# Reordering cross attention's first two rounds: one value product, the additions and the roundings change places

## The reference, cut to what matters

```python
x = x + _L2_ffn_ref(_layernorm(x), ...)      # F
x = x + _L3_xattn_ref(_layernorm(x), ctx_2048, ...)   # G

# F: rows quantised to 255 levels, ternary weights, a bias
scale = jnp.maximum(jnp.max(jnp.abs(x), -1, keepdims=True), eps) / 127.0
q_x = jnp.clip(jnp.round(x / scale), -128.0, 127.0) * scale
return jnp.einsum('bsi,oi->bso', q_x, q_w) + bias

# G: its input is normalised a second time, divided by four vectors of scales
# (for q, qx, k, v) and rounded to fp8; 8 groups g of two heads
ln_out = _ln(hidden_states, ln_w, ln_b)
q  = _ln(_fp8_linear_pertensor(ln_out, wq,  wq_scale,  q_in_scale), qln_w, qln_b)
k  = _ln(_fp8_linear_pertensor(ln_out, wk,  wk_scale,  k_in_scale), kln_w, kln_b)
v  =     _fp8_linear_pertensor(ln_out, wv,  wv_scale,  v_in_scale)
qx = _ln(_fp8_linear_pertensor(ln_out, wqx, wqx_scale, qx_in_scale), qxln_w, qxln_b)
kx, vx = jnp.split(jnp.einsum('bsi,oi->bso', cond, w_kv_x), 2, axis=-1)
cat = concatenate([_gqa(q, k, v), _gqa(qx, kx, vx)])
return jnp.einsum('bsi,oi->bso', _div_clamp_fp8(cat, proj_smooth), wproj) * ...
```

## Time and profile before

| | |
|---|---|
| median of 3 runs | 1086.16 us (1083.81 to 1086.54) |
| the profiled execution's own time | 1085.14 us |
| its span, first to last instruction | 1083.3 us |
| mean granted TensorE clock | 0.987 |
| busy: PE, DVE, ACT, POOL | 1021.9, 868.9, 621.1, 560.1 us |
| round 0's linear products start | 529.12 us |
| round 1's | 550.86 us |
| round 2's | 574.83 us |
| round 3's | 592.02 us |

### The profile page before, as it was taken

The page is one execution under the profiler, slowest core; times in us unless marked ns, Lnnn a source line. Parts: engine busy times, 40 slices in busy tenths (PEclk is TensorE's granted clock), DMA queues, the critical chain, the costliest instruction groups (busy, mean ns, idle before and its releaser), DMA issues.

```text
span 1083.3 us, 19032 instructions
## 1 busy us (share of the span) xinstructions
PE 1021.9 (94%) x6538; PEld 872.1 (80%) x6538; DVE 868.9 (80%) x2154; ACT 621.1 (57%) x1661; POOL 560.1 (52%) x409
## 2 busy tenths in 40 slices
PE   8999999999998899889877999999999999999988
PEld 7458888888887787556556888998889988998976
DVE  6467777767778867789999889888987889888885
ACT  1774444444333347777566756775767666675643
POOL 4247666678653233135156664656555664655540
PEclk9999999999999999899989999999999999999999
DMA  7002101011100012000001101020100101000201
GB/s 272 1 21 93 59 30 59 31 59 40 49 1 28 0 57 77 3 2 2 21 1 42 38 1 41 1 60 1 40 1 21 39 1 40 1 21 1 89 1 40
DMA packets 15007, 37.43 MB, mean 35 GB/s; under 512 B 1648, under 2 KB 6848, under 8 KB 14400
## 3 DMA queue, kind: packets, MB, share of 16 engines
q1 hardware_dynamic: 14912, 36.21, 10.1%
HBM read 35.16 MB, written 1.05 MB: 33 GB/s over the span
## 4 chain that ended last, share of the span: by engine, by line
PE 65%; DVE 20%; ACT 7%; issue 3%; POOL 3%; DMA 0%; DVEq 0%; SPq 0%; ACTq 0%; POOLq 0%
PE bank L743 16%; PE bank L765 8%; PE bank L2213 8%; PE bank L2190 8%; PE bank L2121 7%; PE bank L2096 3%; PE bank L2132 3%; ACT y L2338 3%; PE bank L1128 2%; DVE bst L249 1%; PE bank L2110 1%; DVE y L286 1%; PE bank L531 1%; DVE g_ql L2055 1%; PE bank L532 1%
## 5 line engine op out<-in xcount | busy, mean ns | idle before, releaser
L2338 ACT ACTIVATE y<-bank,g_mx 128x256 f32<-128x256 f32 x256 | 117.2, 484 | 97.8 <-DVE g_mx L2508 97.8
L2623 POOL TENSOR_TENSOR y<-y,g_sm 128x1024 f32<-128x1024 f32 x64 | 120.1, 1896 | 23.9 <-DVE g_sm L2521 23.9
L2599 POOL TENSOR_TENSOR g_c<-arena 128x1024 fp32r<-128x1024 f32 x30 | 64.1, 2135 | 116.4 <-DVE arena L2442 116.4
L2213 PE MATMUL bank<-arena 128*128 128x256 f32 x512 | 116.0, 379 | 0.0
L795 ACT ACTIVATE arena<-arena 128x512 f32<-128x512 f32 x64 | 40.4, 632 | 120.6 <-DVE arena L880 120.5
L2213 PEld LDWEIGHTS bank<-arena 128*128 128x128 f32 x512 | 94.9, 190 | 12.0 <-issue 0.2
L743 PE MATMUL bank<-b_yh,b_wh 128*128 128x512 f32 x256 | 100.6, 393 | 0.0
L743 PE MATMUL bank<-b_yl,b_wh 128*128 128x512 f32 x256 | 100.0, 390 | 0.0
L743 PE MATMUL bank<-b_yh,b_wl 128*128 128x512 f32 x256 | 99.7, 389 | 0.0
L2096 PE MATMUL bank<-cst,y 128*128 128x128 f32 x512 | 74.0, 277 | 17.9 <-DVE x L2430 14.7
L831 POOL TENSOR_TENSOR b_hl<-arena,b_hh 128x512 fp32r<-128x512 f32 x64 | 81.3, 1291 | 9.6 <-ACT b_hh L804 9.6
(11 more groups left out here) (387 smaller groups left out, 3140.0 us busy)
## 6 DMA issues: line engine op xcount, KB each, us to landing
arena<-in_dram SPq DMA_DIRECT2D x37, 512.0 KB, 3.6
arena<-in_dram SPq DMA_DIRECT2D x18, 256.0 KB, 4.0
arena<-in_dram SPq DMA_DIRECT2D x3, 1024.0 KB, 4.9
arena<-in_dram SPq DMA_DIRECT2D x2, 704.0 KB, 7.2
x<-in_dram SPq DMA_DIRECT2D x4, 256.0 KB, 5.4
cx<-in_dram SPq DMA_DIRECT2D x4, 256.0 KB, 5.5
cxT<-in_dram SPq DMA_DIRECT2D x4, 256.0 KB, 5.8
cx<-in_dram SPq DMA_DIRECT2D x1, 1024.0 KB, 8.2
```

The costliest lines, as they stand in the source:

```text
L2213: m = pe.matmul(o[:, st * 256:st * 256 + 256], g_t[:, c, st * P:st * P + P], keys, start=True, stop=True)
L2338: m = act.activation(g_p[:, c, st, :], o[:, st * 256:st * 256 + 256], ACT.Exp, bias=g_mx[j % 2][:, 2 * c + st:2 * c + st + 1], accum_out=g ...
L2599: pool.tensor_tensor(cat, g_o[j % 2], g_om, ALU.subtract).then_inc(s_gc, 1)
L2623: pool.tensor_tensor(pf, pf, sums, ALU.mult).then_inc(s_gp, 1)
```

## The change

Nothing is computed otherwise; instructions of rounds 0, 1 and (for one) 2 change places.

```diff
--- before.py
+++ after.py
@@ -1918,7 +1918,7 @@
         G_TRANSPOSES = (("pt", 0), ("tr", 0), ("pt", 1), ("tr", 2), ("tr", 1), ("pt", 2), ("pt", 3))
         CROSS = [tuple(("V", b, n // 2, n % 2) for n in range(4)) for b in range(B)]
         G_AHEAD = {0: CROSS[1], 1: (("G", "yt", 2),)}
-        G_EXTRA = {0: (("F", "t", 2), ("F", "o", 2)) + CROSS[2] + (("F", "t", 3), ("F", "o", 3)),
+        G_EXTRA = {0: (("F", "t", 2), ("F", "o", 2)) + CROSS[2][0:3] + (("F", "t", 3), CROSS[2][3], ("F", "o", 3)),
                    1: (("G", "yt", 3),) + CROSS[3]}
         for i in range(NG + 3):
             for what, c in G_TRANSPOSES:
@@ -2227,8 +2227,9 @@
                 if i == 0:
                     F_t_pe(pe, 2)
                     F_o_pe(pe, 2)
-                    cross_v_pe(pe, 2, g_wvx[:, 0, :], g_wvx[:, 1, :])
+                    cross_v_pe(pe, 2, g_wvx[:, 0, :], g_wvx[:, 1, :], range(3))
                     F_t_pe(pe, 3)
+                    cross_v_pe(pe, 2, g_wvx[:, 0, :], g_wvx[:, 1, :], (3,))
                     F_o_pe(pe, 3)
                 if i == 1:
                     yt_pe(pe, K_G, "G", (3,))
@@ -2323,8 +2324,9 @@
                                                  scale=row("s_v")), ("G", "kv", i, tt))
                 if i == 0:
                     F_qT_act(act, 2)
-                    cross_v_act(act, 2)
-                    split_p_act(act, 0)
+                    cross_v_act(act, 2, range(3))
+                    F_qT_act(act, 3)
+                    cross_v_act(act, 2, (3,))
                 if i == 1:
                     G_yt_act(act, 3)
                 if 0 <= i - 1 < NG:
@@ -2357,7 +2359,7 @@
                         G_ob_act(act, j, a)
 
                 if i == 0:
-                    F_qT_act(act, 3)
+                    split_p_act(act, 0)
                 if i == 1:
                     G_scale_act(act, 3)
                     cross_v_act(act, 3)
@@ -2510,8 +2512,11 @@
                 if i == 0:
                     ln_scale(dve, K_F, 3)
                     F_quant_dve(dve, V, 3)
-                if i in (1, 2):
-                    G_round_dve(dve, V, i + 1, (i - 1,))
+                    F_bias_dve(dve, V, 3)
+                if i == 1:
+                    G_round_dve(dve, V, 2)
+                if i == 2:
+                    G_round_dve(dve, V, 3, (1,))
                 for tt in range(2):
                     if 0 <= i - 1 < NG:
                         j = i - 1
@@ -2533,18 +2538,15 @@
                         empty(dve.tensor_tensor(g_n[:, tt * 5:tt * 5 + 4, :], o[:, :].rearrange("p (h d) -> p h d", d=P),
                                                 rs4, ALU.mult), ("G", "q", i, tt))
                 if i == 0:
-                    G_round_dve(dve, V, 1, (0,))
                     F_add_dve(dve, V, 2)
                     ln_open_batch(dve, V, 2)
+                    G_round_dve(dve, V, 1, (0,))
+                    ln_scale(dve, K_G, 2)
                     G_round_dve(dve, V, 1, (1,))
-                    ln_scale(dve, K_G, 2)
-                    F_bias_dve(dve, V, 3)
                     F_add_dve(dve, V, 3)
                     ln_open_batch(dve, V, 3)
                     split_p_dve(dve, 0)
                     ln_scale(dve, K_G, 3)
-                if i == 1:
-                    G_round_dve(dve, V, 2, (1,))
                 if i == 2:
                     centre_w_dve(dve, V, 1)
                 if i == 3:
@@ -2608,8 +2610,8 @@
                     C.sync()
                     pool.tensor_tensor(r_, r_, mhalf[:, 0:10], ALU.pow).then_inc(s_grs, 1)
                 if i == 0:
+                    ln_pool(pool, C, K_G, EPS, twice=True, batches=(2,))
                     G_round_pool(pool, 1, (0,))
-                    ln_pool(pool, C, K_G, EPS, twice=True, batches=(2,))
                     G_round_pool(pool, 1, (1,))
                     ln_pool(pool, C, K_G, EPS, twice=True, batches=(3,))
                 if i == 1:
```

## The result

Over 20 runs each, taken in turn, the changed kernel has a median of 1085.78 us (1084.81 to 1088.42) and the kernel before 1084.12 (1081.82 to 1086.98); the ratio is 1.0017, with a 95% interval of 1.0010 to 1.0024. So by the ratio the change costs 1.8 us (1.1 to 2.6): it is slower, and by less than 0.3%. The forecast was +2.3 us. Its 1088.4 us lay higher than the 1085.78 measured mainly because the kernel before's own median came down from 1086.16 in the three runs shown to 1084.12 in twenty.

The account below looks back on a forecast made before the run. PE was taken to bound the kernel, but not rounds 0 and 1, where DVE and POOL delay its start. 2.71 + 0 - 0.43 = +2.28 us, carried whole: 1088.4 us on the median, range 1084.4 to 1091.3.

Parts of the forecast that it names:

- First part, the row of DVE in round 0: Round 0: DVE's new order up to the second rounding delays POOL's subtractions and PE's round 1 start by 2.71 us.
- The products on PE and ACT: Rounds 0 and 1: PE's swapped products and ACT's split projection fall ahead of the wait for `g_xs`, so worth 0.
- The clock: Round 1's linear products: PE again at the low clock, the same 6.27 us, so 0; bounds 2.33 less, 0.3 more.
- Rival 2: PE's clock stays at 2.4 GHz into round 1's linear products; sum -1.3 us, 1084.8 us; chance 0.15.
- Second part, round 1: DVE's new order in round 1: last maximum to PE's round 2 start takes 13.00 us for 13.43, -0.43.
- The lock taken to the letter: DVE and POOL: an exclusive port lock blocks the later one for whole instructions; sum +3.4 us in place of +2.3.
- The carry: From round 2 on both orders are alike, so the +2.28 us reaches the end whole.
- Rival 3: PE's 14.7 us of slack behind 600 us absorbs the delay; 1086.2 us; chance 0.12.
- rival 1: Both locks cost in full and PE's clock falls again in round 1; +4.9 us, 1091.1 us; chance 0.25.
- The signs named beforehand: PE's round 1 products near 553.6 after about 5 us idle, transposes L340 near 547.8, round 2 near 577.1.

Follow-up runs that it names:

- e1: The changed kernel with the order of DVE and POOL in round 0 put back as before; ratio to the kernel before 0.9993 (0.9981 to 1.0004).
- e4: The kernel before with only the change's moves on PE and ACT; ratio to the kernel before 0.9989 (0.9979 to 1.0000).
- e3: The changed kernel with only batch 3's bias put back behind the second rounding; ratio to the kernel before 1.0008 (0.9997 to 1.0019).
- e5: The changed kernel with POOL's first pair of subtractions in round 1 moved behind its multiplications; ratio to the kernel before 1.0026 (1.0015 to 1.0037).
- e7: e6 with DVE also doing batch 2's second pair of subtractions in round 1; ratio to the kernel before 1.0014 (1.0003 to 1.0025).
- after_again: The changed kernel measured once more, nothing altered; ratio to the kernel before 1.0024 (1.0014 to 1.0034).
- e6: e1 with DVE doing batch 1's last two subtractions in round 0, batch 2's transposes and scaling later; ratio to the kernel before 1.0001 (0.9988 to 1.0014).
- e9: e8 with DVE also doing batch 1's second pair of subtractions in round 0, PE's order kept; ratio to the kernel before 0.9992 (0.9981 to 1.0002).
- e8: e1 with DVE doing batch 2's second pair of subtractions in round 1; ratio to the kernel before 0.9990 (0.9981 to 0.9999).

## Why the prediction was right

*First part, the row of DVE in round 0: predicted +2.71 us, measured +2.55.* The row itself is exact: 11.24 us for the 11.24 that the sum gives (539.70 to 550.94). Its scaling took 1.57 (1.56 expected) and the delayed first instruction 1.38 (0.42 + 0.95). The 0.15 that is missing lies behind it: POOL's last subtractions took 2.27 us and not 2.42, since DVE's next instructions, F's addition and moments, left them alone. That the loss comes from the order of DVE and POOL in round 0, and not from PE's and ACT's moves, is shown by e1, which takes PE's start back to 21.74, and by e4. That it is not the row's length alone is shown by e3: a row 0.74 us shorter brought PE's start forward by 0.35, since POOL's subtractions grew by 0.38.

*The products on PE and ACT: 0, right for the start of round 1.* F's last product starts 13.4 us behind round 0's products for 15.8, and all of it came back as idle time; in e4's trace the moves alone leave round 1's start at 21.74. What the term leaves out is the clock, through which e4 and e1 seem to win about 1 us over many executions; with the whole change the mean granted clock over twenty executions is 0.9885, so nothing of it is seen there.

*The clock: 0, measured +0.17.* Most of the linear products ran at 1.2 GHz, 6.44 us for 6.27. Rival 2, that the clock would stay high, did not come.

*Second part, round 1: predicted -0.43, measured -0.45.* The sum is right, its terms for the second rounding and for POOL are not. The second rounding took 4.19 us and not 3.81: both of POOL's subtractions hit it, 0.83 each, and I had taken 1.3 for the two. POOL's multiplications took 3.70 from start to start (3.74 in their row) for the 3.92 and its subtractions 2.27 for the 2.46. I had taken both from rows with a rounding of DVE's beside them; here two normalisations and a copy out of a PSUM bank stood beside the multiplications and took their usual 0.66 and 0.69, and of a rounding only the first instruction met the last subtraction (and took 1.03 for 0.42). The errors are +0.38 and -0.41. This is luck, and a better sum would have asked of each POOL duration as well what ran beside it in the old order.

*The lock taken to the letter*, that each of the two subtractions stops DVE for its whole length, would have given 2.27 us of delay; e5 measures 1.67. The rule of the Trainium skill ("SBUF — State Buffer", section "SBUF: two separate sides") holds in kind, as e5 and e7 show; its size here is 0.83 for a subtraction of 1.28. Of that, 0.29 us was over when DVE's instruction started (565.92 and 566.21); the other 0.16 is not explained.

*The carry: whole, right.* +2.27 at round 2, +2.33 at round 20, +2.32 at the end. Rival 3 is out. So is rival 1, which asked for steps of 2.9 and 0.5 us and a clock that falls again in round 1: the steps are 2.55 and -0.45, and the granted clock from 572.20 to 576.20 is 1.00.

*The signs named beforehand.* They are on the clock of the old trace, which this execution runs 0.87 us ahead of. With 0.87 added, the transposes L340 start at 547.68 (near 547.8 was named), round 1's products at 553.41 (near 553.6) after 5.10 us of waiting for POOL, and round 2's at 577.10 (near 577.1). `g_xs` of batch 1 was finished at 552.49 as read, and at 553.36 on the old clock, so not before 552.5. Maximum to start took 12.98 us, between 12 and 14.

*Level.* 2.55 + 0.17 - 0.45 = 2.27 us in the profiled executions; the ratio over all runs gives 1.8 (1.1 to 2.6), that of after_again 1.0024, or 2.6 us (1.5 to 3.7).

## What to carry to other kernels

When two chains end within 0.1 us of each other, moving an instruction ahead of the end of one lengthens that chain, however long the wait that it removes in the other; write both ends down before moving anything. The cost is up to the instruction's full length: the bias, 0.72 us in the row, was worth 0.35 at PE's start (e3). On VectorE and GpSimd a row's duration is a duration in company: before reusing it in another place, see what the other engine did beside it. And an order that makes TensorE early without making its next input early buys an idle stretch (4.13 us in e6, 2.96 in e9), which can be paid for a second time in the clock.

## What was not expected of the hardware

- TensorE's clock makes two executions of the same work differ by nearly as much as the change does. Ahead of round 0, where all kernels here are alike, PE idles 2.0 us before its transposes L340. In e1 it then took four value instructions of L1999 and L2000 in 1.92 and 1.76 us, in e8 in 1.02 and 1.02, and from L1546 to round 0's products went 14.49 us in e1 and 12.77 in e8. What e8 won there was lost at round 1's wait. The 32 matmuls of round 1 took 4.81 to 6.60 us over the runs here, at a mean granted clock of 0.79 and 0.54; how much of that spread is the order and how much the execution is open, but the changed kernel's two traces have 6.44 and 6.47. Over the 31 executions of the kernel before in the group of e5 to e7 the time is 0.57 us shorter for each 0.001 that the mean granted clock is higher (correlation -0.85), so most of the scatter of 5 us goes with the clock.
- VectorE delays GpSimd too, though by less than the other way round: a pair of subtractions took 2.27 us with F's addition and moments beside it, 2.42 beside the scaling, 2.46 to 2.57 beside roundings, 2.65 beside the bias. Two multiplications took 3.74 beside the normalisations and 4.19 beside VectorE's subtractions, which themselves took 3.66 for 1.29.
